# Turning the expert weights of three batches on the DMA queue instead of on TensorE, in a decoder kernel

## The reference, cut to what matters

```
x = x + attention(layernorm(x))     # Wqk, Wv, Wu, Wo: 512 x 512 each, 16 heads of 32
x = x + experts(layernorm(x))       # 4 experts chosen by token id; gate = up = down = ctx_2048[e]
x = x + ffn(layernorm(x))           # ternary W_up, W_gate, W_down: 2048 x 512, split by mean(|W|)

q = k = elu(heads(n @ Wqk + bqk)); v = silu(n @ Wv + bv); u = silu(n @ Wu + bu)
attention = (u * layernorm(q @ (k^T v))) @ Wo + bo
experts   = (silu(n @ C^T) * (n @ C^T)) @ C^T        # C = ctx_2048[e], a 512 x 512 matrix
```

## Time and profile before

| | us |
|---|---|
| median of 3 runs | 686.11 (684.96 to 686.34) |
| the profiled execution's own time | 685.89 |
| its span in the trace | 684.1 |
| TensorE busy in it | 667.0 (97%) |
| VectorE, ScalarE, POOL busy | 512.2, 294.6, 211.1 |

### The profile page before, as it was taken

The page is one execution under the profiler, slowest core; times in us unless marked ns, Lnnn a source line. Parts: engine busy times, 40 slices in busy tenths (PEclk is TensorE's granted clock), DMA queues, the critical chain, the costliest instruction groups (busy, mean ns, idle before and its releaser), DMA issues.

```text
span 684.1 us, 11895 instructions
## 1 busy us (share of the span) xinstructions
PE 667.0 (97%) x4498; PEld 434.5 (64%) x4498; DVE 512.2 (75%) x818; ACT 294.6 (43%) x440; POOL 211.1 (31%) x221
## 2 busy tenths in 40 slices
PE   8999999999999989999999999999999999999996
PEld 5456556556547575555556777777777777777772
DVE  6676873865755769999886987787878986776665
ACT  4475654545536344564332534342433434332331
POOL 4113713213135220000320443326343644324222
PEclk8999999999999999999999999999999999999999
DMA  7947039018215466883331111113020221101001
GB/s 195 374 148 238 1 117 252 0 61 234 74 61 183 143 209 216 243 229 84 67 55 28 28 28 28 28 28 90 1 55 2 44 73 28 28 1 62 1 1 61
DMA packets 78963, 65.00 MB, mean 95 GB/s; under 512 B 59200, under 2 KB 59200, under 8 KB 77888
## 3 DMA queue, kind: packets, MB, share of 16 engines
q1 hardware_dynamic: 76352, 55.89, 29.9%
q0 software_dynamic: 2560, 8.42, 3.5%
HBM read 42.51 MB, written 8.41 MB: 74 GB/s over the span
## 4 chain that ended last, share of the span: by engine, by line
PE 84%; DVE 7%; DMA 3%; issue 2%; ACT 1%; POOL 1%; SPq 1%; POOLq 0%; DVEq 0%; ACTq 0%
PE bank L1310 33%; PE bank L1602 28%; PE bank L1611 15%; PE bank L1303 3%; DVE region L889 3%; PE bank L1482 2%; PE bank L1468 2%; DVE late L885 1%; PE bank L1504 1%; DMA stage<-in_L_ffn_W_up_dram 1%; DMA late<-n 1%; ACT tmp L559 1%; DVE region L893 1%; DMA sorted_residual<-rows,pos 1%; DVE st L744 0%
## 5 line engine op out<-in xcount | busy, mean ns | idle before, releaser
L1602 PE MATMUL bank<-w_att,region 128*128 128x256 f16 x1024 | 127.6, 273 | 0.0
L1611 PE MATMUL bank<-region,w_moe 128*128 128x512 bf16 x512 | 120.3, 379 | 0.8 <-DVE w_moe L1220 0.8
L1602 PEld LDWEIGHTS bank<-w_att,region 128*128 128x128 bf16 x1024 | 100.1, 98 | 18.2 <-DVE tmpA L1235 0.2
L1310 PE MATMUL bank<-late,w_att 128*128 128x512 f16 x384 | 87.0, 381 | 1.4 <-DVE region L939 1.0
L1231 DVE TENSOR_TENSOR n<-bank,n 128x512 f32<-128x512 f32 x112 | 71.4, 684 | 19.0 <-PE bank L1602 17.1
L473 POOL TENSOR_TENSOR w_moe<-tmp,w_moe 128x512 f16<-128x512 f32 x30 | 39.2, 1306 | 139.0 <-ACT w_moe L709 139.0
L1611 PEld LDWEIGHTS bank<-region,w_moe 128*128 128x128 f16 x512 | 50.0, 98 | 48.8 <-DVE w_moe L1220 1.3
L702 ACT ACTIVATE n<-n,qs 128x512 f32<-128x512 f32 x64 | 44.5, 719 | 64.7 <-DVE n L1231 64.7
L1602 PE MATMUL bank<-w_att,late 128*128 128x256 f16 x512 | 66.4, 273 | 0.0
L1310 PEld LDWEIGHTS bank<-late,w_att 128*128 128x128 f16 x384 | 37.3, 99 | 44.6 <-DVE region L939 1.7
L1602 PEld LDWEIGHTS bank<-w_att,late 128*128 128x128 bf16 x512 | 50.0, 98 | 12.1
(11 more groups left out here) (171 smaller groups left out, 1073.7 us busy)
## 6 DMA issues: line engine op xcount, KB each, us to landing
stage<-in_L_ffn_W_up_dram SPq DMA_DIRECT2D x8, 1024.0 KB, 6.9
stage<-in_L_ffn_W_gate_dram SPq DMA_DIRECT2D x8, 1024.0 KB, 6.3
rows<-sorted_residual SPq DMA_DIRECT2D x16, 257.5 KB, 3.0
stage<-in_ctx_dram SPq DMA_DIRECT2D x4, 1024.0 KB
stage<-in_L_ffn_W_down_dram SPq DMA_DIRECT2D x4, 1024.0 KB
nrm<-in_L_ffn_W_down_dram SPq DMA_DIRECT2D x4, 1024.0 KB, 8.4
rows<-in_x_dram SPq DMA_DIRECT2D x1, 3072.0 KB, 16.1
rows<-in_x_dram SPq DMA_DIRECT2D x4, 256.0 KB, 3.7
```

The costliest lines, as they stand in the source:

```text
L1310: mm = pe.matmul(dst, lhs(*step), rhs(*step), start=(start and n == 0), stop=(stop and n == len(steps) - 1))
L1602: mm = pe.matmul(wk_ps[bank][:, q * H:(q + 1) * H], w[:, c + q, k * P:(k + 1) * P], x3S_part[slot][:, h, m, k], start=(h == 0 and k == 0), ...
L1611: mm = pe.matmul(ffy_ps[t][:, :], hid[:, u, h, q, (t % 2) * P:(t % 2 + 1) * P], tern[2][:, c + q], start=(begins and q == 0 and h == 0), s ...
```

## The change

For batches 1 to 3 TensorE no longer turns the expert matrix. ScalarE splits the whole of `stage[:, 0]` in row order in one instruction of 2048 columns (`ctx_half_hi`, after `v_act(b, 3)` and ahead of `magnitudes(b, 0)`), VectorE makes the remainders in four of 512 (`ctx_half_lo`, after the second residual sum and the statistics behind it), both into `x_half`, and SyncE turns each with one DMA transpose into `w_moe` (`weights_turned`), which stands in SyncE's queue ahead of the wait for `magnitudes(b, 0)`. `half_hi` and `half_lo` of the next batch now wait for these two transposes. Batch 0 keeps the transposes on TensorE.

Beside it:
- POOL adds a batch's biases after its fourth value sum (`v_bias`), not after its first.
- In batch 0 the four query products go to four banks and don't wait for `q_elu`, and VectorE splits the value weights (L796) ahead of the first `q_elu`.
- `keep_busy`: 58 for 46 at the start, 7 new ones after each of the first three transposes of the first norm, none after the first two query products; in the tail 14 and 66 for 52 and 16.
- VectorE makes the second half of the first unit's signs ahead of `last_sum(3)`, not behind it, and SyncE loads unit (1, 0) when these are made, ahead of its wait for the scattered rows.

```diff
+        def weights_turned(b):
+            if b == B - 1:
+                sp.wait_ge(s["route_ready"], 3)
+            for h in range(2):
+                if h:
+                    sp.wait_ge(s["ctx_half_lo"], T * b)
+                else:
+                    sp.wait_ge(s["ctx_half_hi"], b)
+                sp.dma_start_transpose(out=w_moe[:, b, h].rearrange("p k (r s) -> p (k r) s", s=P), in_=x_half[:, h]).then_inc(
+                    s["ctx_in"], 16)
+
         def weights(b):
 
+            if b > 0:
+                weights_turned(b)
             sp.wait_ge(s["abs_done"], 3 * b + 1)
             summed_unit(b, 1)
...
             if b > 0 and b + 1 < B:
-                sp.wait_ge(s["ctx_mm"], 4 * b + 4)
                 expert_weights(b + 1)
...
+        sp.wait_ge(s["sign_b"], 1)
+        unit(1, 0)
         sp.wait_ge(s["scattered"], 16 * NT)
...
-            pool.wait_ge(s["v_bias"], T * b + 1)
+            pool.wait_ge(s["v_bias"], T * b + T)
...
+        def ctx_half_hi(b):
+            act.wait_ge(s["stage_in0"], 16 * b + 16)
+            act.wait_ge(s["half_hi_in"], 16 * b)
+            act.activation(ctx_out[:, 0], ctx_blocks, ACT.Copy, scale=CTX_SCALE).then_inc(s["ctx_half_hi"], 1)
...
-                ctx_hi(b, 1)
+                ctx_half_hi(b)
                 magnitudes(b, 0)
...
+        def ctx_half_lo(b):
+            dve.wait_ge(s["half_lo_in"], 16 * b)
+            dve.wait_ge(s["ctx_half_hi"], b)
+            for r in range(T):
+                dve.scalar_tensor_tensor(out=ctx_out[:, 1, r], in0=ctx_blocks[:, r], scalar=CTX_SCALE, in1=ctx_out[:, 0, r],
+                                         op0=ALU.mult, op1=ALU.subtract).then_inc(s["ctx_half_lo"], 1)
...
                 for t in range(T):
                     residual(b - 1, t)
                     if t < 2 and not last:
                         first_stats(b + 1, (2 * t, 2 * t + 1))
-                ctx_lo(b, 2)
+                    if t == 1:
+                        ctx_half_lo(b)
...
+        two_signs(0, True)
         last_sum(3)
-        two_signs(0, True)
...
-                if not first and m == 1:
-                    pe.wait_ge(s["stage_in0"], 16 * b + 16)
-                    ctx_part(b, 0)
...
-                ctx_part(b, 1)
                 project(b - 1, T * b + 3)
...
-                if not first and t == 1:
-                    ctx_part(b, 2)
...
-                    elif not first and m == 0:
-                        ctx_part(b, 3)
```

More of the change, by code:

```diff
@@ L143, in decoder @@
     x_turned = xT.rearrange("p i k (t s) -> p i (k t) s", s=P)
+    ctx_blocks = stage[:, 0].rearrange("p r (k s) -> p r k s", s=P)
+    ctx_out = x_half.rearrange("p h (k r s) -> p h r k s", k=K, r=T)
     half_out = x_half.rearrange("p h (k t s) -> p h t k s", k=K, t=T)
@@ L296, in next_tile @@
             sorted_tile(i)
-        next_unit(0)
         for i in range(3, 6):
@@ L558, in batch @@
                     act.wait_ge(s["q_elu"], K * b + m - 1)
-                act.activation(tmp[:, m % 2], acc[m % 2][:, :], ACT.Exp, bias=cols[:, 0, m:m + 1]).then_inc(s["q_exp"], 1)
+                bank = four_banks[m] if first else acc[m % 2]
+                act.activation(tmp[:, m % 2], bank[:, :], ACT.Exp, bias=cols[:, 0, m:m + 1]).then_inc(s["q_exp"], 1)
             if first:
@@ L588, in batch @@
                     v_act(b, T - 1)
-                elif not first and t == 1:
-                    ctx_hi(b, 2)
             if first:
@@ L933, in ctx_lo, with q_elu @@
                                      op1=ALU.subtract).then_inc(s["ctx_lo"], 1)
-        def q_elu(b, m):
+        def q_elu(b, m, bank=None):
+            bank = acc[m % 2] if bank is None else bank
             dve.wait_ge(s["q_exp"], K * b + m + 1)
@@ L938, in q_elu @@
             dve.wait_ge(s["q_clip"], K * b + m + 1)
-            dve.scalar_tensor_tensor(out=qT[:, m], in0=acc[m % 2][:, :], scalar=cols[:, 0, m:m + 1],
+            dve.scalar_tensor_tensor(out=qT[:, m], in0=bank[:, :], scalar=cols[:, 0, m:m + 1],
                                      in1=tmp[:, m % 2], op0=ALU.add, op1=ALU.max).then_inc(s["q_elu"], 1)
@@ L951, in batch @@
             dve.wait_ge(s["o_mm"], T * b)
-            q_elu(b, 0)
-            q_elu(b, 1)
             if first:
                 split(1)
-            else:
+                for m in range(K):
+                    q_elu(b, m, four_banks[m])
+            else:
+                q_elu(b, 0)
+                q_elu(b, 1)
                 head_norm(b - 1)
-            q_elu(b, 2)
-            q_elu(b, 3)
+                q_elu(b, 2)
+                q_elu(b, 3)
             dve.wait_ge(s["kv_mm"], 2 * b)
@@ L1001, in batch @@
                 first_norm(b + 1, True)
-            ctx_lo(b, 3)
+                ctx_lo(b, 3)
             if not last:
@@ L1053, in last_sum @@
         def last_sum(t):
-            residual(B - 1, t, last_bank)
+            residual(B - 1, t, four_banks)
             second_stats(B - 1, t)
@@ L1326, in first_norm @@
                 transposes(first_bank[t], lambda k: nrm[:, t, k * P:(k + 1) * P]).then_inc(s["t1_mm"], 1)
+                if t < T - 1:
+                    keep_busy(kv_ps, 7)
         def ctx_part(b, k):
@@ L1347, in operands @@
                 cut = slice(t * P, (t + 1) * P)
-                bank = last_bank[t] if bank_free is None else acc[t % 2]
+                bank = four_banks[t] if bank_free is None else acc[t % 2]
                 return bank[:, :], lambda i, j, k: aT[:, i, k, cut], lambda i, j, k: w_att[:, 3, j, k]
@@ L1381, in query @@
             def query(m):
-                return (acc[m % 2][:, :], lambda i, j, k: w_att[:, 0, j, k, m * P:(m + 1) * P], lambda i, j, k: xT[:, i, k])
+                return ((four_banks[m] if first else acc[m % 2])[:, :], lambda i, j, k: w_att[:, 0, j, k, m * P:(m + 1) * P], lambda i, j, k: xT[:, i, k])
             if first:
@@ L1400, in batch @@
                     pe.wait_ge(s["u_act"], K * (b - 1) + 3 + m)
-                else:
+                elif not first:
                     pe.wait_ge(s["q_elu"], K * b + m - 1)
@@ L1421, in batch @@
                 if t < 2:
-                    pe.wait_ge(s["q_elu"], K * b + 3 + t)
+                    pe.wait_ge(s["q_elu"], K * b + (1 if first else 3) + t)
                 else:
@@ L1436, in batch @@
                     if first:
-                        pe.wait_ge(s["x_lo"], 3 + t)
+                        pe.wait_ge(s["q_elu"], K)
                     else:
@@ L1449, in batch @@
             pe.wait_ge(s["w_lo"], 3)
-            if last:
-                ctx_part(b, 3)
-            else:
+            if not last:
                 for m in range(K):
@@ L1508, in _ @@
         pe.wait_ge(s["pool_const"], 1)
-        keep_busy(kv_ps, 46)
+        keep_busy(kv_ps, 58)
         pe.wait_ge(s["ident_made"], 1)
@@ L1530, in _ @@
         pe.wait_ge(s["x1_done"], T * (B - 1) + 1)
-        keep_busy(ps[0], 52)
+        keep_busy(ps[0], 14)
         unit_transposes(0, 0)
-        keep_busy(ps[0], 16)
+        keep_busy(ps[0], 66)
         unit_transposes(0, 1)
@@ L1588, in expert_step @@
             return off
+        pe.wait_ge(s["ctx_in"], 32 * (B - 1))
         pe.wait_ge(s["route_ready"], 3)
```

19 lines of the change are left out of this document (5 added, 14 removed).

## The result

The changed kernel takes 692.48 us, the median of its runs (692.35 to 693.22), against 685.54 (684.04 to 686.34) for the kernel before on the same chip: a ratio of 1.0098 [1.0081, 1.0116], 1% slower. The profiled execution took 692.35 with a span of 690.6, 6.5 longer than before. The forecast had the direction and the place, and 4.5 us too little.

The account below looks back on a forecast made before the run. TensorE, busy 97% of the span, was taken as the bound. Terms +3.6 - 0.4 - 0.5 - 1.3 - 0.85 - 0.2 = +0.35, plus 1.6 for the clock, gave 687.8, as a median 688.0 us; range 684.2 to 692.0.

Parts of the forecast that it names:

- The removed transposes and POOL's move: Batches 1 to 3: without transposes ahead and with POOL's biases later, the projection starts 0.9 us sooner per batch.
- The late unit: Batches 1 and 2: unit (b, 1), loaded behind both turned halves, stalls TensorE 3.1 us before the third gate product.
- The clock: Behind each 3.1 us gap TensorE's clock may fall, costing 3.4 us; taken as 0.8 each, 1.6 together.
- Rival 1: Batches 1 and 2: the clock holds through the 3.1 us gaps; 686.5 us, no change; chance 0.28.
- rival 3: Batches 1 and 2: the clock falls long both times; +7.2, 693.3 us; chance 0.15.
- (d): Tail: with unit (1, 0) there, `h32` waits for ScalarE alone, 0.85 us sooner.
- (e): Tail: signs ahead of `last_sum(3)` cost 0.6 us, POOL's root returns 1.0; -0.2, between -0.4 and +1.
- Batch 3: Last batch: the projection gives 0.9 us and the key-value products 0.4, together -1.3.
- No gate product is near: nothing: Batch 3: the late unit delays magnitudes, but only head copies wait behind them, so it costs nothing.
- Batch 0: First batch: values start 1 to 2 us sooner, but the first unit's load limits the gain; -0.5 us.
- Rival 4: POOL's additions only move onto other VectorE work and the value sum stays late; 689.4 us; chance 0.07.
- rival 2: Batches 1 and 2: unit (b, 1) lands in time for the third gate product; 681.3 us; chance 0.12.

Follow-up runs that it names:

- experiment 11: Experiment 6 with unit (b, 1) late again as in the changed kernel, the gap filled with 54 matmuls on ones: 686.91 us.
- experiment 12: Experiment 6 with unit (b, 1) late again as in the changed kernel, the gap not filled: 689.73 us.
- experiment 2: The changed kernel with unit (1, 0) loaded back behind the first three sorted rows, signs still ahead of the last residual sum: 692.28 us.
- experiment 6: Experiment 5 with POOL's biases of batch 0 added after the first value sum, as in the kernel before: 680.59 us.
- experiment 10: Experiment 6 with signs ahead of the last residual sum and `keep_busy` at 14 and 66, unit (1, 0) still behind the sorted rows: 682.27 us.
- experiment 5: Experiment 1 with the whole tail as in the kernel before: 680.98 us.
- experiment 9: The kernel before with the change's batch 0 edits and POOL's move in batches 1 to 3, weights still turned on TensorE: 684.77 us.
- experiment 8: Experiment 6 with both signs of the first unit ahead of the first residual sum, unit (1, 0) loaded then, `keep_busy` at 14 and 66: 681.33 us.
- experiment 1: The changed kernel with SyncE loading unit (b, 1) between the two turned halves: 683.69 us.
- experiment 3: The changed kernel with 54 matmuls on ones filling the gap ahead of the third gate product in batches 1 and 2: 690.46 us.
- experiment 4: The kernel before with POOL's biases after the fourth value sum in all batches: 687.88 us.

## Why the prediction was right or wrong

**The removed transposes and POOL's move: right.** In batch 1 the projection starts 1.33 sooner, less batch 0's 0.41: 0.92, and 0.9 was forecast. Batch 2 gained 1.21, of which 0.28 is the wait for turned rows inside its first queries, gone with the change. The source was POOL beside VectorE, as argued: the two remainders L889 of the earlier trace rows, 3.25 together, are 0.68 and 0.69 now.

**The late unit: right, with two errors that cancel in part.** The gap is 3.18 for 3.1. SyncE was free 0.5 sooner than forecast, and the load took 6.2 us from issue to use where 5.2 was taken.

**The late unit: right, to 0.2 us at every step but one**, as the timeline above has it. The one is the unit behind the transposes: from issue to use it took 6.2 (94.34 to 100.52), not the 5.2 forecast (12.9 to 18.1), while SyncE came to it 0.5 sooner. The extra for a load behind a transpose was taken as 0.5 and measured 1.5 over the 4.7 of the earlier trace rows. The Trainium skill, "DMA: Bandwidth & Descriptors", in its table of behaviours, has 261 GB/s for DMA transposes, by which that extra would be nothing; the trace does not agree. Net of clock, 1.7 and 1.1 per batch against 1.6.

**The clock: the step that failed, by its size.** "I take half of it in half of the cases" made 1.6. The two gaps cost 4.6 in the profiled execution and 2.8 on the median of experiments 11 and 12. Each fall seen behind these gaps is 1.4 to 3.0 of lost time, and by the mean granted clock of the runs they come in most executions. The reason given, that dense work behind the gap would cut the fall short, does not hold: batch 2's fall lasted 6.8 us under work without a gap, as long as that of the earlier trace rows under sparse work. Rival 1 (the clock holds) was seen in one profiled execution, experiment 2; rival 3 (long both times) in no profile. What decides between a fall and none at the same 3.2 us of idle time stays open. The kernel before varies with its clock too: of its 56 runs beside the experiments, the 22 with a mean granted clock of 0.998 or more have a median of 685.1, the 14 with 0.995 or less one of 686.9. The Trainium skill, "TensorE: Matmul & The Clock Gate", Part 1, has a long enough idle stretch put the array back to 1.2 GHz; of the gaps near 3 us in these traces most agree and experiment 2's two do not.

**The tail, (d) and (e): failed, in sign.** Forecast -0.85 and -0.2; measured +2.7 on the median. (d)'s own row came true (the wait for `h32` is 0.54, was 1.41). With the unit loaded late it is 0.54 in experiments 6 and 10, but 0.9 to 1.4 in 2, 5, 9, 11 and 12: the earlier load gives between nothing and 0.9. (e) looked at the last row alone, and there it was right: against experiment 6 the last scatter of experiment 10 leaves 0.4 sooner, once the 0.67 by which its first scatter is late is taken off. What it left out is that the scatters queue behind one another. From the third scatter's issue to the fetch of the sorted rows it takes, in us:

| kernel | third to fourth issue | third issue to fetch |
|---|---|---|
| before | 3.3 | 6.8 |
| 5, 6 and 11 | 3.3 | 6.9, 6.8, 6.5 |
| 8 | 1.9 | 6.8 |
| 2 and 10 (new order, late load) | 2.0 | 6.8, 7.2 |
| after, 1 and 3 (new order, early load) | 2.0 | 7.7, 8.1, 8.7 |

Without the early load the landing keeps to 6.5 to 7.2 behind the *third* issue, however soon the fourth follows. The signs put the third row's root from 0.57 to 1.41 and its scatter 0.8 later; the last row, which they were moved past, had slack. The load of 1 MB, issued beside the last scatters, then adds 0.9 to 1.9 (none in 8, where it is issued earlier), over the upper bound of +1 that (e) had for it. That the scatters form a queue is what the table suggests; the traces list no single scatter's traffic. The later rows also lengthen TensorE's wait ahead of the first expert tile from 0.39 to between 1.5 and 3.3 with the new order, and in the profiles of 1, 3 and 10 the clock fell behind it, which (e) had not priced at all.

**Batch 3: right as a sum (-1.2 for -1.3), wrong in one part.** "No gate product is near: nothing" was false. ScalarE's magnitudes, held up by the late unit, put the third gate product back too:
```profile
216.58 1.91 ACT L570 ACTIVATE stage<-stage 128x2048 f32<-128x2048 f32 x1 [3.06 <-DMA stage<-in_L_ffn_W_gate_dram]
...
227.14 2.76 PE L1329 MATMUL bank<-late,w_att 128*128 128x512 f16 x12 [0.48 <-ACT region L629]
```
(all engines, changed kernel). That is 0.5 lost. It is made up at the projection, which starts 1.5 sooner against the batch's queries, not 0.9.

**Batch 0: right in size (-0.4 for -0.5), by luck.** The values start at 23.28, at 26.12 before: 2.8 sooner, 1 to 2 was forecast. Some 1.2 of it is the clock, which does not fall at the start of the changed kernel's profile (an estimate, from experiment 4, whose code is that of before up to there). Nearly all of the 2.8 is lost again, and part of that loss the forecast did not have. Rival 4 was at work in this batch: POOL's biases moved onto VectorE's small copies. VectorE's timeline of the changed kernel, and then TensorE's:
```profile
35.14 1.05 DVE L839 COPY region<-region 128x4 f32<-128x4 f32 x1
...
38.53 1.13 DVE L839 COPY region<-region 128x32 f32<-128x32 f32 x1
```
```profile
41.25 0.66 PE L1322 MATMUL bank<-ident,stage 128*128 128x128 f32 x4 [1.28 <-DVE w_moe L950]
```
The copies took 0.17 before. In experiments 6, 8, 10, 11 and 12, with POOL's biases of batch 0 back in their old place, they take 0.17 again and the wait of 1.28 is gone, so it came from the move. But the batch ends at 57.8 to 58.8 there, and at 58.5 to 58.7 in the changed kernel and experiments 1, 2, 3 and 5: other waits take its place, 0.76 for VectorE and up to 1.36 for the load of the expert's matrix. So the move costs 2.4 in the kernel before (experiment 4), and 0.4 on the median beside the new split order (experiment 6), within the spread.

**The range** of 684.2 to 692.0 missed by 0.5, on the side where it left out a tail that costs. It was said to take in half of rival 2 and most of rival 3, but ended short of the times given for both, 681.3 and 693.3. The two errors, 3.0 of clock in the profiled execution and 1.7 of tail, have one root: a change was priced at the place where it stands, and what it sets off behind that place (a lower clock, a queue of scatters) was taken as small.

## What to carry to other kernels

When work moves onto a DMA queue, walk through what stands behind it in that queue: here one load moved ahead of a transpose that would have waited anyway turned 1.0% slower into 0.3% faster. Price a new TensorE gap of about 3 us at its length plus some 1.4 us for the clock (half of the 2.8 of experiments 11 and 12), and fill it with matmuls nobody reads if it can't be closed. Where several scatters or loads run in a row, look for the one that sets the landing before making room for the last.

## What was not expected of the hardware

- The same kernel, with the same gaps of 3.18 and 3.06 us, ran once with no clock fall (688.81) and otherwise at 692.1 to 693.6. Falls came in two lengths, some 3.4 and 6.8 us. Behind waits in the tail of 2.03, 2.80 and 3.34 the clock fell, behind one of 2.33 in the changed kernel it did not.
- Beside POOL's additions VectorE's small copies of 128x4 and 128x32 took 1.05 and 1.13 instead of 0.17, while the small additions between them, 128x60 to 128x48, kept their 0.20 to 0.21. POOL's four additions took 4.60 with VectorE mostly reading banks, 6.25 beside its remainders.
- SyncE came free of the two turned halves 8.97 us after it took the first, waits included, and a 1 MB load issued then was usable 6.2 us later, against about 4.7 without them (an estimate, from the issue in the earlier trace rows and the end of traffic in the earlier trace rows).
